# First routing of a two-layer mixture-of-experts kernel: one group of tiles per stage instead of one group per step, unrolled

## The chip, the cores and the metric

One core of one Trainium2 chip. The metric is device time in microseconds (us) of one execution. Engines: TensorE (PE; its weight loads are PEld), VectorE (DVE), ScalarE (ACT), GpSimd (POOL), and SyncE (SP), which only issues DMAs here. A trailing q (SPq, POOLq) is the queue of that engine.

## What is computed

```python
x = x + conv7x7_depthwise(ln_c(x))             # 16 x 128 x 24 x 24
t = tokens(x)                                  # 9216 tokens of 128
t = t + moe_0(ln_t(t))                         # 8 experts, top 2, 128 -> 512 -> 128, silu
x = x + filtered_leaky_relu(ln_c(from_tokens(t)))   # FIR up by 2, leaky ReLU, FIR down by 2
t = t + moe_1(ln_t(tokens(x)))                 # 8 experts, top 2, gated, 128 -> 256 -> 128

def moe_0(x):                                  # x: tokens x 128
    top_logits, top_idx = top_k(x @ Wg, 2)
    w = softmax(top_logits)                    # 2 weights per token
    return sum over the 2 experts e: w_e * silu(x @ W1[e]) @ W2[e]
```

The change concerns how `moe_0` finds, for every token, its two experts and its two rows in a table sorted by expert.

## The kernel before

Six stages follow each other, each behind a barrier of all engines: the first convolution, the first routing (`route0_phase`), the experts of layer 0, the second convolution with the second routing woven in (`conv1_phase`), the experts of layer 1, and the sum of the answers. The first routing is the stage between about 255 and 545 us of the trace.

It handles 20 **groups** of tokens (`GROUPS`): 4 image groups `ig` times 5 strips `q`, group number g = 5 ig + q. A group is 120 partitions (96 for q = 4) times 4 tiles of 128 features. The work on one group:

- SP loads it with one DMA per image row (L677): 5 of 48 KB, 4 where q = 4. The groups 0 to 4 are loaded first, then the constants `factor_a`, `factor_b`, `down`, `down_b` and the weights `w1l`, `w` (L682, L382, L383), then the groups 5 to 19. Group g waits until group g-5 is normalised.
- **measure**, DVE, L404 to L409: mean and variance. ACT takes the root (L416).
- **apply**, DVE, L424, L478, L431: reciprocal, the copy of the destinations into the row buffer `xn`, and the normalised rows. `xn` has 5 places, one per q, so group g waits until the scatters of group g-5 have landed (`scattered`). ACT copies the rows for the second expert (L489).
- **transposes and logits**, PE L498, ACT L507, PE L517.
- **pick**, DVE, L529 to L540: the two largest logits, their indices (L532), a cast of the indices to floats in `at` (L535), the one-hot form (L536), `picked` (L538). `gap` (L533) goes to ACT, which takes its exponential (L548). A different table is loaded by ACT for the root and for the exponential (ACT_TABLE_LOAD). PE then ranks the tokens (L557 to L561).
- **place**, DVE, L571 to L582: weights and row numbers (`slot`); its last act, at L583, frees POOL.
- POOL **scatters** the group: 8 DMA_INDIRECT instructions (L594), one per tile and choice.

What sets the order is the order of writing on each in-order engine. In step g DVE does measure g, pick g-1, apply g, place g-1, and each engine runs 5 steps as a loop body (`groups`: step 0 to 4 written out, then a loop over `ig`). Every DVE instruction that reads what the one ahead of it wrote waits on a semaphore that this one raises (`Chain`). After the last step DVE computes `factor_a` (L756), places the last group, makes the table of blocks (`route_make_table`, L610 to L638), and computes `down` (L759), `gl` (L761) and `w1l` (L763). ACT copies `w1h` (L710) and `gh` (L712) after its last step.

`conv1_phase` uses the same functions `norm_measure`, `norm_scale`, `norm_apply` and `route_pick`.

Of the kernel before, what the change touches and what calls it, by code (L numbers as in the profile page):

```python
# [28 lines left out]
P = 128  # L29
# [12 lines left out]
NORM_STEPS, PICK_STEPS, PLACE_STEPS = 3, 6, 4  # L42
# [344 lines left out]
class Norm:  # L387


    def __init__(self, nc, ctx, sem, name, eps):  # L390
        sb = lambda n, s: ctx.enter_context(nc.sbuf_tensor(f"{name}_{n}", s, F32))
        self.nc, self.eps = nc, eps
        self.stats, self.mv = sb("stats", [P, IG, 6]), sb("mv", [P, IG, 2])
        self.rstd = sb("rstd", [P, IG])
        self.chain, self.beat = sem(f"{name}_chain"), sem(f"{name}_beat")
        self.var_ready, self.std_ready, self.applied = (sem(f"{name}_{n}") for n in ("var", "std", "applied"))


def norm_measure(m, dve, ig, q, x):

    nc, px, g = m.nc, pixels(q), QT * ig + q
    ch = Chain(dve, m.chain, NORM_STEPS * g)
    for t in range(IG):
        ins = nc.vector.bn_stats(m.stats[0:px, t, :], x[:, t, :])  # L404
    ch.after(ins, m.beat)
    for t in range(IG):
        ins = nc.vector.bn_aggr(m.mv[0:px, t, :], m.stats[0:px, t, :])
    ch.after(ins)
    nc.vector.tensor_scalar(m.rstd[0:px], m.mv[0:px, :, 1], m.eps, None, ALU.add).then_inc(m.var_ready, 1)  # L409


def norm_root(m, act, ig, q):

    px = pixels(q)
    need(act, m.var_ready, QT * ig + q + 1)
    m.nc.scalar.activation(m.rstd[0:px], m.rstd[0:px], ACT.Sqrt).then_inc(m.std_ready, 1)  # L416


def norm_scale(m, dve, ig, q):

    nc, px, g = m.nc, pixels(q), QT * ig + q
    ch = Chain(dve, m.chain, NORM_STEPS * g + 2)
    need(dve, m.std_ready, g + 1)
    ch.after(nc.vector.reciprocal(m.rstd[0:px], m.rstd[0:px]))  # L424


def norm_apply(m, dve, ig, q, out, x):

    px = pixels(q)
    for t in range(IG):  # L430
        ins = m.nc.vector.tensor_scalar(out[:, t, :], x[:, t, :], m.mv[0:px, t, 0:1], m.rstd[0:px, t:t + 1],  # L431
# [4 lines left out]
class Router:  # L436


    def __init__(self, nc, ctx, sem, r, layer, xs):
# [3 lines left out]
        self.norm = Norm(nc, ctx, sem, f"ln{layer}", 1e-5)  # L443
# [3 lines left out]
        self.at, self.gap, self.ex, self.den = sb("at", [P, CHOICES]), sb("gap", [P, IG]), sb("ex", [P, IG]), sb("den", [P, IG])  # L447
# [74 lines left out]
def route_pick(ro, dve, ig, q):  # L522
# [8 lines left out]
    for t in range(IG):  # L531
# [124 lines left out]
def route0_phase(nc, io, r, wt, xs, src):  # L656

    with ExitStack() as ctx:
        sem = ctx.enter_context(stage_semaphores(nc, "r0_"))
        ro = Router(nc, ctx, sem, r, 0, xs)  # L660
# [7 lines left out]
        LAST = (IMAGE_GROUPS - 1, QT - 1)  # L668
# [20 lines left out]
        def _(act):  # L689
# [9 lines left out]
            def step(ig, q):  # L699
                last = before(ig, q)  # L700
                norm_root(ro.norm, act, ig, q)
                if last:
                    route_exponent(ro, act, *last)
                route_copy_rows(ro, act, ig, q)
                route_copy_turned(ro, act, ig, q)
# [17 lines left out]
        def _(pe):  # L723
# [3 lines left out]
            def step(ig, q):  # L727
                last = before(ig, q)
                if last:
                    route_ranks(ro, pe, *last)  # L730
# [661 lines left out]
```

## Time and profile before

| | us |
|---|---|
| median of the timed runs | 1649.24 |
| lowest and highest of the 3 runs | 1646.86, 1649.58 |
| span of the profiled execution | 1726.5 |
| GpSimd busy in it | 699.3 |
| VectorE busy in it | 1106.1 |
| TensorE busy in it | 1207.4 |

The page of the profile describes one execution, whose span runs from the first to the last instruction. It is 77.3 us longer than the median of the timed runs. Idle time of an engine is put down to the event that came last before the engine went on; "issue" and "remote" are waits for which the trace shows no releasing instruction, and a name such as `c_meanw` beside such a wait is that of an older owner of the same semaphore. Rows give the start and the duration in us; "x4" says that four like instructions are merged.

### The profile page before, as it was taken

What the parts mean: (1) busy time and instruction counts of PE and PEld (TensorE: products, weight loads), DVE (VectorE), ACT (ScalarE), POOL (GpSimd) and SP (SyncE); (2) the same over time, 40 slices, a digit from 0 to 9 for tenths busy, and PEclk for the clock granted to TensorE, in tenths of its full rate; (3) what the DMA queues carried; (4) which work ended last, traced back from release to release, by engine and by line L of the source; (5) the groups of instructions that cost most, each with busy time, mean ns of one, the idle gap of its engine ahead of it and who ended that gap; (6) DMA issues with size and microseconds to landing.
All of it is one profiled execution on the core that took longest, in us unless ns stands there. A gap on an engine that the chain in (4) does not pass through costs nothing. (4 is left out here: it accounts for less than half of the span.)

```text
span 1726.5 us, 31708 instructions
## 1 busy us (share of the span) xinstructions
PE 1207.4 (70%) x6568; PEld 956.4 (55%) x6569; DVE 1106.1 (64%) x4125; ACT 587.5 (34%) x1099; POOL 699.3 (41%) x680
## 2 busy tenths in 40 slices
PE   4799903223222999999946979889797089999940
PEld 4799902212122999998934545455454067777730
DVE  7677704434345666666648688787876467777754
ACT  4233303323231444444432234334344134444320
POOL 0100005565574444444434045345554535555530
PEclk9899955555555999999976989989898589999975
DMA  4033297121111222222232011121011122222239
GB/s 200 22 107 106 64 121 273 53 58 55 39 44 46 66 62 62 62 63 60 62 128 79 1 46 51 28 58 42 26 32 31 40 73 74 75 79 71 73 103 261
DMA packets 139200, 129.26 MB, mean 75 GB/s; under 512 B 56291, under 2 KB 119012, under 8 KB 138214
## 3 DMA queue, kind: packets, MB, share of 16 engines
q1 hardware_dynamic: 89396, 79.76, 16.9%
q0 software_dynamic: 19968, 39.44, 7.0%
q10 hardware_dynamic: 29778, 9.45, 2.7%
q14 instruction: 41, 0.34, 0.1%
q8 instruction: 17, 0.28, 0.1%
HBM read 78.66 MB, written 50.99 MB: 75 GB/s over the span
## 5 line engine op out<-in xcount | busy, mean ns | idle before, releaser
L594 POOL DMA_INDIRECT routed<-r_xn,r_slot x320 | 333.3, 1042 | 346.6 <-DVEq L583 233.9
L823 POOL DMA_INDIRECT answers<-e_y,e_dest x304 | 291.1, 958 | 347.1 <-ACT e_y L922 272.9
L972 DVE COPY e_ht<-e_ps_ht 128x512 f32<-128x512 f32 (+1 forms) x304 | 169.5, 558 | 180.9 <-PE e_ps_ht L859 156.7
L867 PE MATMUL e_ps_y<-w,e_ht 128*128 x1824 | 258.6, 278 | 13.4 <-DVE e_ht L972 7.4
L867 PEld LDWEIGHTS e_ps_y<-w,e_ht 128*128 128x128 f32 x1824 | 228.6, 192 | 20.1 <-issue 18.8
L1135 PE MATMUL c_pz<-c_c,down 116*120 116x512 f32 (+1 forms) x392 | 199.7, 627 | 0.0
L922 ACT ACTIVATE e_y<-e_ps_y,e_weight 128x128 f32<-128x128 f32 x304 | 111.8, 368 | 217.7 <-issue 117.9
L859 PE MATMUL e_ps_ht<-ident,e_h 128*128 128x128 f32 x912 | 150.8, 274 | 6.0 <-DVE e_h L958 5.5
L849 PE MATMUL e_ps_h<-w1h,e_xl 128*128 x308 | 150.9, 490 | 1.1 <-issue 0.7
L1109 PE MATMUL c_py<-c_xh,gl 121*116 121x512 f32 (+1 forms) x196 | 124.1, 633 | 39.1 <-DVE c_xl L1215 27.1
L859 PEld LDWEIGHTS e_ps_ht<-ident,e_h 128*128 128x128 f32 x912 | 115.4, 141 | 56.0 <-DVE e_h L958 10.7
L557 PE MATMUL r_ps_rank<-r_picked,before 120*120 120x32 bf16 (+1 forms) x40 | 9.9, 248 | 177.7 <-DVEq L539 150.1
L842 PE MATMUL e_ps_x<-ident,e_xg 128*128 128x128 f32 x310 | 86.0, 277 | 67.3 <-DMA e_xg<-routed 67.3
L1171 ACT ACTIVATE c_a<-c_py 116x512 f32<-116x512 f32 x116 | 69.0, 595 | 184.9 <-PE c_py L1109 159.0
L851 PE MATMUL e_ps_h<-w1h,e_xh 128*128 x308 | 123.5, 401 | 0.0
L850 PE MATMUL e_ps_h<-w1l,e_xh 128*128 x308 | 122.8, 399 | 0.0
L1223 DVE SCALAR_TENSOR_TENSOR c_c<-c_a 116x512 f32<-116x512 f32 x116 | 86.9, 749 | 52.1 <-ACT c_a L1171 41.1
L917 ACT ACTIVATE e_h<-e_ps_h 128x512 f32<-128x512 f32 x154 | 92.0, 597 | 61.1 <-PE e_ps_h L851 60.5
L557 PEld LDWEIGHTS r_ps_rank<-r_picked,before 120*120 120x120 bf16 (+1 forms) x40 | 6.1, 152 | 186.3 <-DVEq L539 155.3
L498 PE MATMUL r_ps_t<-ident,r_xn 120*128 120x120 f32 (+1 forms) x160 | 35.0, 362 | 95.3 <-DVE r_xn L431 83.3
L1135 PEld LDWEIGHTS c_pz<-c_c,down 116*120 116x120 f32 (+1 forms) x392 | 70.2, 187 | 52.5 <-issue 43.6
L950 DVE TENSOR_TENSOR e_xl<-e_ps_x,e_xh 128x128 fp32r<-128x128 f32 x310 | 90.3, 291 | 10.7
(134 smaller groups left out, 2445.4 us busy)
## 6 DMA issues: line engine op xcount, KB each, us to landing
e_xg<-routed SPq DMA_DIRECT2D x318, 66.0 KB
answers<-answers SPq DMA_DIRECT2D x32, 480.0 KB
c_w<-in_w SPq DMA_DIRECT2D x32, 448.0 KB
c_x<-in_xh SPq DMA_DIRECT2D x4, 1536.0 KB
routed<-r_xn,r_slot POOLq DMA_INDIRECT x320
answers<-e_y,e_dest POOLq DMA_INDIRECT x304
x<-x SPq DMA_DIRECT2D x96, 48.0 KB
w1l<-in_w SPq DMA_DIRECT2D x2, 2048.0 KB, 10.3
```

The source lines that it names most:

```text
L594: ro.nc.gpsimd.indirect_dma_start(ro.xs, bass.IndirectOffsetOnAxis(ap=ro.slot[0:px, q, c:c + 1], axis=0), ro.xn[0:px, q, k, t, :], None).t ...
L823: nc.gpsimd.indirect_dma_start(ys, bass.IndirectOffsetOnAxis(ap=dest[:, s:s + 1], axis=0), y[:, s, :], None).then_inc(stored[s], 16)
L849: nc.tensor.matmul(ps_h[i][:], xl[:, i, :], wt.w1h[:, bass.ds(w, FF)], start=True, stop=False)
L850: nc.tensor.matmul(ps_h[i][:], xh[:, i, :], wt.w1l[:, bass.ds(w, FF)], start=False, stop=False)
L851: nc.tensor.matmul(ps_h[i][:], xh[:, i, :], wt.w1h[:, bass.ds(w, FF)], start=False, stop=True).then_inc(h_ready, 1)
L859: ins = nc.tensor.transpose(ps_ht[s % 2][:, c * P:(c + 1) * P], h[:, s % 2, c * P:(c + 1) * P], r.ident[:])
L867: ins = nc.tensor.matmul(ps_y[s % 2][:, 0:P], ht[:, s % 2, c * P:(c + 1) * P], wt.w2[:, bass.ds(w + c * P, P)], start=c == 0, stop=c == ch ...
L917: nc.scalar.activation(h[:, i, :], ps_h[i][:], ACT.Silu).then_inc(hid_ready, 1)
L922: nc.scalar.activation(y[:, s % U, :], ps_y[s % 2][:, 0:P], ACT.Copy, scale=weight[:, s % U:s % U + 1]).then_inc(y_ready, 1)
L972: nc.vector.tensor_copy(ht[:, s % 2, :], ps_ht[s % 2][:, 0:HID]).then_inc(ht_ready, 1)
L1109: ins = nc.tensor.matmul(out, w[0:k, wcols], v, start=start and n == 0, stop=stop and n == 2)
L1135: ins = nc.tensor.matmul(ps_z[q % 3][0:rows, :], r.down[0:PPX, m * TPX:m * TPX + rows], c[0:PPX, p % R, :], start=p == ROWS * q, stop=p == ...
```

## The change

The steps of the stage are written out, 24 of them (20 groups and 4 to empty the pipeline), for every engine but SP, and in turn n each part works on another group: measure n, apply n-1, place n-4, pick n-3 on DVE; root n, copies of n-1, exponential of n-3 on ACT; transposes of n-1, logits of n-2, ranks of n-3 on PE. Since measure now runs a group ahead of apply, the norm's `mv` and `rstd` have two places in the first routing. The constants and weights are computed inside turns 12 to 14 instead of after the last step. In both routings the cast into `at` is gone: the one-hot form compares with the integer indices, in a view of 4 dimensions. The reciprocal of the norm has a semaphore of its own.

```diff
-        self.stats, self.mv = sb("stats", [P, IG, 6]), sb("mv", [P, IG, 2])
-        self.rstd = sb("rstd", [P, IG])
+        self.stats, self.mv = sb("stats", [P, IG, 6]), sb("mv", [P, ring, IG, 2])
+        self.rstd = sb("rstd", [P, ring, IG])
...
-    ch.after(nc.vector.reciprocal(m.rstd[0:px], m.rstd[0:px]))
+    nc.vector.reciprocal(m.rstd[0:px, i], m.rstd[0:px, i]).then_inc(m.inverted, 1)
+    need(dve, m.inverted, g + 1)
...
-    ch.after(nc.vector.tensor_copy(ro.at[0:px].rearrange("p (t k) -> p t k", k=2), ro.top_at[0:px, :, 0:2]))
-    ch.after(nc.vector.tensor_tensor(ro.onehot[0:px].rearrange("p t k e -> p (t k) e"), ro.r.iota8[0:px],
-                                     ro.at[0:px].unsqueeze(2).to_broadcast([px, CHOICES, EXPERTS]), ALU.is_equal))
+    ch.after(nc.vector.tensor_tensor(ro.onehot[0:px], ro.r.iota8[0:px].rearrange("p (t k) e -> p t k e", k=2),
+                                     ro.top_at[0:px, :, 0:2].unsqueeze(3).to_broadcast([px, IG, 2, EXPERTS]), ALU.is_equal))
...
+        APPLY, LOGITS, PICK, PLACE = 1, 2, 3, 4
+        WEIGHTS_AT = 12
+        def lagged(n, lag):
+            return [divmod(n - lag, QT)] if 0 <= n - lag < GROUPS else []
...
         @block.scalar
...
-            groups(act, step)
-            route_exponent(ro, act, *LAST)
-            act.wait_ge(w_in, 32)
-            nc.scalar.activation(wt.w1h[:], wt.w1f, ACT.Copy).then_inc(w_split, 1)
-            act.wait_ge(g_ready, 1)
-            nc.scalar.activation(r.gh[:], fa[:], ACT.Copy).then_inc(gh_ready, 1)
+            for n in range(GROUPS + PLACE):
+                for ig, q in lagged(n, 0):
+                    norm_root(ro.norm, act, ig, q)
+                for ig, q in lagged(n, APPLY):
+                    route_copy_rows(ro, act, ig, q)
+                    route_copy_turned(ro, act, ig, q)
+                for ig, q in lagged(n, PICK):
+                    route_exponent(ro, act, ig, q)
+                if n == WEIGHTS_AT:
+                    act.wait_ge(w_in, 32)
+                    nc.scalar.activation(wt.w1h[:], wt.w1f, ACT.Copy).then_inc(w_split, 1)
+                if n == WEIGHTS_AT + 1:
+                    act.wait_ge(g_ready, 1)
+                    nc.scalar.activation(r.gh[:], fa[:], ACT.Copy).then_inc(gh_ready, 1)
...
         @block.gpsimd
...
-            groups(pool, lambda ig, q: route_scatter(ro, pool, ig, q))
+            for n in range(GROUPS):
+                route_scatter(ro, pool, *divmod(n, QT))
...
         @block.tensor
...
-            groups(pe, step)
-            route_ranks(ro, pe, *LAST)
+            for n in range(GROUPS + PLACE):
+                for ig, q in lagged(n, APPLY):
+                    route_turn(ro, pe, ig, q)
+                for ig, q in lagged(n, LOGITS):
+                    route_logits(ro, pe, ig, q)
+                for ig, q in lagged(n, PICK):
+                    route_ranks(ro, pe, ig, q)
...
         @block.vector
...
-            groups(dve, step)
-            route_pick(ro, dve, *LAST)
-            dve.wait_ge(factors_in, 64)
-            nc.vector.scalar_tensor_tensor(fa[:], fa[:], 4.0, fb[:], ALU.mult, ALU.mult).then_inc(g_ready, 1)
-            route_place(ro, dve, *LAST)
+            for n in range(GROUPS + PLACE):
+                for ig, q in lagged(n, 0):
+                    need(dve, x_in[q], 16 * (pixels(q) // SIDE) * (ig + 1), ro.norm.beat)
+                    norm_measure(ro.norm, dve, ig, q, r.x[0:pixels(q), QT * ig + q])
+                for ig, q in lagged(n, APPLY):
+                    norm_scale(ro.norm, dve, ig, q)
+                    route_normalise(ro, dve, ig, q)
+                for ig, q in lagged(n, PLACE):
+                    route_place(ro, dve, ig, q)
+                for ig, q in lagged(n, PICK):
+                    route_pick(ro, dve, ig, q)
+                if n == WEIGHTS_AT:
+                    dve.wait_ge(w_split, 1)
+                    nc.vector.tensor_tensor(wt.w1l[:], wt.w1f, wt.w1h[:].bitcast(F32), ALU.subtract)
+                    dve.wait_ge(factors_in, 64)
+                    nc.vector.scalar_tensor_tensor(fa[:], fa[:], 4.0, fb[:], ALU.mult, ALU.mult).then_inc(g_ready, 1)
+                    nc.vector.tensor_tensor(r.down[:], r.down[:], down_b[:], ALU.mult)
+                if n == WEIGHTS_AT + 2:
+                    dve.wait_ge(gh_ready, 1)
+                    nc.vector.tensor_tensor(r.gl[:], fa[:], r.gh[:].bitcast(F32), ALU.subtract)
             route_make_table(ro, dve)
...
```

Two places in the order of DVE's instructions. The first is its start in the stage, before: measure 0 (above the piece), apply 0, measure 1, pick 0 (from L529), and, a few rows on, place 0 (from L571), which frees the first scatter.

```order
L424 RECIPROCAL ln_rstd<-ln_rstd 120x4
L478 COPY r_xn<-dest 120x8
L431 TENSOR_SCALAR r_xn<-x,ln_mv,ln_rstd 120x128 x4
L404 BN_STATS ln_stats<-x 120x6 x4
L407 BN_AGGR ln_mv<-ln_stats 120x2 x4
L409 TENSOR_SCALAR ln_rstd<-ln_mv 120x4
L529 MAX r_top<-r_ps_l 120x8 x4
L532 MAX_INDEX r_top_at<-r_top,r_ps_l 120x8 x4
L533 TENSOR_TENSOR r_gap<-r_top 120x4
L535 CAST r_at<-r_top_at 120x8
```

In the changed kernel the same pick 0 (L536 to L546 there) stands behind measure 0 to 3 and apply 0 to 2, and measure 4 (96 partitions) and apply 3 stand between it and place 0 (from L577); the piece begins at the end of pick 0.

```order
L546 TENSOR_REDUCE r_group_sum<-r_picked 120x8
L410 BN_STATS ln_stats<-x 96x6 x4
L413 BN_AGGR ln_mv<-ln_stats 96x2 x4
L415 TENSOR_SCALAR ln_rstd<-ln_mv 96x4
L430 RECIPROCAL ln_rstd<-ln_rstd 120x4
L485 COPY r_xn<-dest 120x8
L438 TENSOR_SCALAR r_xn<-x,ln_mv,ln_rstd 120x128 x4
L577 TENSOR_SCALAR r_den<-r_ex 120x4
L580 TENSOR_TENSOR r_earlier<-r_earlier,r_group_sum 120x8
```

So place 0 moved behind three more measures and two more applies, and place 1 now stands behind measure 5. The second place is the end of turn 12 on DVE, after: behind pick 9 stand the three long instructions that before came after the last step, and then measure 13.

```order
L546 TENSOR_REDUCE r_group_sum<-r_picked 96x8
L766 TENSOR_TENSOR w1l<-w1l,w1h 128x4096
L768 SCALAR_TENSOR_TENSOR factor_a<-factor_a,factor_b 128x1624
L769 TENSOR_TENSOR down<-down,down_b 128x1200
L410 BN_STATS ln_stats<-x 120x6 x4
```

Place 9 comes only after them, in turn 13.

## Rows read from the trace of the kernel before

**Rows 1.** The page's summary line.
```profile
span 1726.5 us, 31708 instructions
```

**Rows 2.** Groups of instructions by line, POOL, 255 to 545 us: busy, mean ns, idle before.
```profile
L594 POOL DMA_INDIRECT routed<-r_xn,r_slot x160 | 166.5, 1040 | 111.5 <-issue 59.9 <-DVEq L583 51.2 <-DMA routed<-r_xn,r_slot 0.3
```

**Rows 3.** Timeline of POOL: start, duration; in brackets idle before and releaser.
```profile
273.52 1.18 POOL L594 DMA_INDIRECT routed<-r_xn,r_slot  x1 [13.61 <-issue]
...
284.20 0.99 POOL L594 DMA_INDIRECT routed<-r_xn,r_slot  x1 [0.30 <-issue]
...
312.05 0.99 POOL L594 DMA_INDIRECT routed<-r_xn,r_slot  x1 [6.83 <-DVEq L583]
```

**Rows 4.** Timeline of DVE, the first steps of the stage.
```profile
264.36 0.87 DVE L404 BATCH_NORM_STATS2 ln_stats<-x 120x6 f32<-120x128 f32 x4 [0.35 <-DMA x<-x]
...
265.79 0.17 DVE L409 TENSOR_SCALAR ln_rstd<-ln_mv 120x4 f32<-120x4 f32 x1
267.77 0.39 DVE L529 MAX8 r_top<-r_ps_l 120x8 f32<-120x8 f32 x4 [1.81 <-PE r_ps_l L517]
...
269.01 0.17 DVE L535 CAST r_at<-r_top_at 120x8 f32<-120x8 uint32 x1
...
269.94 0.17 DVE L424 RECIPROCAL ln_rstd<-ln_rstd 120x4 f32<-120x4 f32 x1
...
271.24 0.16 DVE L571 TENSOR_SCALAR r_den<-r_ex 120x4 f32<-120x4 f32 x1
...
272.26 0.17 DVE L582 CAST r_slot<-r_slot_f 120x8 int32<-120x8 f32 x1
...
279.50 0.17 DVE L582 CAST r_slot<-r_slot_f 120x8 int32<-120x8 f32 x1
```

**Rows 5.** Timeline of DVE, a later step, while POOL issues its second group in a row.
```profile
403.73 0.38 DVE L407 BATCH_NORM_AGGREGATE ln_mv<-ln_stats 120x2 f32<-120x6 f32 x4 [2.44 <-DMA c_meanw<-in_mean_w]
408.53 0.17 DVE L409 TENSOR_SCALAR ln_rstd<-ln_mv 120x4 f32<-120x4 f32 x1 [4.43 <-DMA c_meanw<-in_mean_w]
```

**Rows 6.** SP's register instructions of line L677: duration ns min/median/max, first and last start.
```profile
L677 SPq FUSED_REGOPS  x72: 4/64/707, 272.5 to 446.7; - x72
```

**Rows 7.** Timeline of SP: the loads of the groups from 5 on, issued behind the weights.
```profile
272.83 54.12 SPq L677 DMA_DIRECT2D x<-x  x29
```

**Rows 8.** Stretches: length, busy PE, PEld, DVE, ACT, POOL, PEclk, DMA share, GB/s.
```profile
288.00:292.00 4.00, 2.69 (x12) 2.22 (x12) 0.29 (x2) 2.32 (x3) 3.00 (x4) 0.50 0.93 295
292.00:296.00 4.00, 0.00 (x0) 0.00 (x0) 1.33 (x7) 0.00 (x0) 2.81 (x3) 0.50 0.36 97
```

**Rows 9.** Timeline of PE and ACT in the second step of the stage.
```profile
272.48 0.57 ACT L507 ACTIVATE r_xnt<-r_ps_t 128x480 f32<-128x480 f32 x1 [0.49 <-PE r_ps_t L498]
...
273.10 1.77 PE L517 MATMUL r_ps_l<-wg,r_xnt 128*120 128x8 f32 x8 [0.66 <-ACT r_xnt L507]
...
274.58 1.28 ACT L548 ACT_TABLE_LOAD   x1
...
276.31 0.20 ACT L548 ACTIVATE r_ex<-r_gap 120x4 f32<-120x4 f32 x1 [0.45 <-DVE r_gap L533]
```

**Rows 10.** Timeline of all engines at the end of the stage.
```profile
510.88 3.60 ACT L710 ACTIVATE w1h<-w1l 128x4096 fp32r<-128x4096 f32 x1
...
511.62 1.84 DVE L756 SCALAR_TENSOR_TENSOR factor_a<-factor_a,factor_b 128x1624 f32<-128x1624 f32 x1
...
529.53 1.39 DVE L759 TENSOR_TENSOR down<-down,down_b 128x1200 f32<-128x1200 f32 x1
530.21 7.60 POOL L594 DMA_INDIRECT routed<-r_xn,r_slot  x1 [0.31 <-issue]
...
530.84 1.83 DVE L761 TENSOR_TENSOR gl<-factor_a,gh 128x1624 fp32r<-128x1624 f32 x1
532.60 4.41 DVE L763 TENSOR_TENSOR w1l<-w1l,w1h 128x4096 fp32r<-128x4096 f32 x1
```

**Rows 11.** Who waited for whom, second convolution and routing, 895 to 1385 us: total, times, longest.
```profile
PE r_ps_rank L557 <- DVEq L539: 29.7, 9, 9.4
```

More of the change, by code:

```diff
@@ L41 @@
 DEST, WEIGHT = P, P + 1
-NORM_STEPS, PICK_STEPS, PLACE_STEPS = 3, 6, 4
+NORM_STEPS, PICK_STEPS, PLACE_STEPS = 2, 5, 4
 CGS, CIN, RPAD = 4, 32, 32
@@ L406, in norm_measure @@
     for t in range(IG):
-        ins = nc.vector.bn_aggr(m.mv[0:px, t, :], m.stats[0:px, t, :])
+        ins = nc.vector.bn_aggr(m.mv[0:px, i, t, :], m.stats[0:px, t, :])
     ch.after(ins)
-    nc.vector.tensor_scalar(m.rstd[0:px], m.mv[0:px, :, 1], m.eps, None, ALU.add).then_inc(m.var_ready, 1)
+    nc.vector.tensor_scalar(m.rstd[0:px, i], m.mv[0:px, i, :, 1], m.eps, None, ALU.add).then_inc(m.var_ready, 1)
 def norm_root(m, act, ig, q):
-    px = pixels(q)
+    px, i = pixels(q), norm_slot(m, QT * ig + q)
     need(act, m.var_ready, QT * ig + q + 1)
-    m.nc.scalar.activation(m.rstd[0:px], m.rstd[0:px], ACT.Sqrt).then_inc(m.std_ready, 1)
+    m.nc.scalar.activation(m.rstd[0:px, i], m.rstd[0:px, i], ACT.Sqrt).then_inc(m.std_ready, 1)
 def norm_scale(m, dve, ig, q):
     nc, px, g = m.nc, pixels(q), QT * ig + q
-    ch = Chain(dve, m.chain, NORM_STEPS * g + 2)
+    i = norm_slot(m, g)
     need(dve, m.std_ready, g + 1)
-    ch.after(nc.vector.reciprocal(m.rstd[0:px], m.rstd[0:px]))
+    nc.vector.reciprocal(m.rstd[0:px, i], m.rstd[0:px, i]).then_inc(m.inverted, 1)
+    need(dve, m.inverted, g + 1)
 def norm_apply(m, dve, ig, q, out, x):
-    px = pixels(q)
+    px, i = pixels(q), norm_slot(m, QT * ig + q)
     for t in range(IG):
-        ins = m.nc.vector.tensor_scalar(out[:, t, :], x[:, t, :], m.mv[0:px, t, 0:1], m.rstd[0:px, t:t + 1],
+        ins = m.nc.vector.tensor_scalar(out[:, t, :], x[:, t, :], m.mv[0:px, i, t, 0:1], m.rstd[0:px, i, t:t + 1],
                                            ALU.subtract, ALU.mult)
@@ L446, in __init__ @@
         self.top, self.top_at = sb("top", [P, IG, 8]), sb("top_at", [P, IG, 8], U32)
-        self.at, self.gap, self.ex, self.den = sb("at", [P, CHOICES]), sb("gap", [P, IG]), sb("ex", [P, IG]), sb("den", [P, IG])
+        self.gap, self.ex, self.den = sb("gap", [P, IG]), sb("ex", [P, IG]), sb("den", [P, IG])
         self.onehot, self.picked = sb("onehot", [P, IG, 2, EXPERTS]), sb("picked", [P, IG, EXPERTS], BF16)
@@ L725, in _ @@
             pe.wait_ge(init, 2)
[L727 to L730, printed above, removed]
-                route_turn(ro, pe, ig, q)
-                route_logits(ro, pe, ig, q)
-            groups(pe, step)
-            route_ranks(ro, pe, *LAST)
+            for n in range(GROUPS + PLACE):
[5 more added lines that the diff above has]
+                    route_ranks(ro, pe, ig, q)
             route_count_all(ro, pe)
@@ L740, in _ @@
             nc.vector.tensor_copy(r.before[:], before_f[:]).then_inc(init, 1)
-            def step(ig, q):
-                last = before(ig, q)
-                need(dve, x_in[q], 16 * (pixels(q) // SIDE) * (ig + 1), ro.norm.beat)
-                norm_measure(ro.norm, dve, ig, q, r.x[0:pixels(q), bass.ds(QT * ig + q, 1)].rearrange("p a t c -> p (a t) c"))
-                if last:
-                    route_pick(ro, dve, *last)
-                norm_scale(ro.norm, dve, ig, q)
-                route_normalise(ro, dve, ig, q)
-                if last:
-                    route_place(ro, dve, *last)
@@ L762, in _ @@
-            dve.wait_ge(w_split, 1)
-            nc.vector.tensor_tensor(wt.w1l[:], wt.w1f, wt.w1h[:].bitcast(F32), ALU.subtract)
+            for n in range(GROUPS + PLACE):
[18 more added lines that the diff above has]
+                    nc.vector.tensor_tensor(r.gl[:], fa[:], r.gh[:].bitcast(F32), ALU.subtract)
```

26 lines of the change are left out of this document (9 added, 17 removed).

## The prediction

> **What bounds the kernel now.** I read the summary first. The profiled span is 1726.5 us [rows 1], the median of the timed runs 1649.24, so the profiled execution is 77.3 us longer than a timed one. An offset of that size matters here: somewhere it holds waits that a timed run may not have, and I had to find where before costing anything.
>
> Then the groups of instructions of the stage that the change rewrites. POOL issues 160 scatters of 1.04 us, and is idle for 111.5 us ahead of them, 51.2 of these for the release by DVE at L583 [rows 2]. The timeline of POOL shows the pattern: eight scatters take 284.20 - 273.52 = 10.7 us for the first group and 8 x (0.99 + 0.30) = 10.3 for a later one, I take 10.4; two groups run back to back, and then POOL stands idle, 6.83 us the first time, until DVE has placed the next [rows 3]. There are 8 such waits (51.2 us, 6.4 each).
>
> Why is DVE late? Its own step is short: place 0 ends at 272.43 and place 1 at 279.67, a step of 7.24 us [rows 4], 3 us less than POOL needs for a group. But while POOL issues its second group in a row, each wait of DVE stretches: 2.44 and 4.43 us on waits whose releaser had long been done [rows 5]. It is not DVE's data. SP, which touches no data, shows the same: register instructions with a median of 64 ns take up to 707 [rows 6]. So in those stretches every sequencer is slow, whatever it does.
>
> Are these stalls in the timed runs? Without them POOL would run through: 273.5 + 20 x 10.4 = 481.5, plus about 9 us in which long instructions of DVE hold it up (below), is 490.5. In the trace the last scatter ends at 530.21 + 7.60 = 537.8 [rows 10]. The stalls cost this stage 47.3 us, and 77.3 have to go somewhere. That is the only candidate of the right size that I find, and the slow waits look like something that comes with recording every instruction. I take it that **in a timed run the first routing is bound by POOL**, which issues without a gap from 273.5 on, and that DVE, PE and ACT have slack of 3 us per group. This is the assumption on which the sign rests.
>
> **The change part by part.**
>
> *The start (adds).* Before, DVE does measure 0, apply 0, measure 1, pick 0, apply 1, place 0. After, place 0 stands in turn 4, behind three more measures and two more applies. From the rows [rows 4]: measure 265.96 - 264.36 = 1.60; apply 271.24 - 269.94 = 1.30; pick 269.94 - 267.77 = 2.17, less the cast 0.20, is 1.97; place 272.43 - 271.24 = 1.19; from there to the first scatter 273.52 - 272.43 = 1.09 [rows 3, 4]. Measure 1 starts at 264.36, when group 1 has come. Turns 1 to 3 then end at 267.26, 270.16 and 275.03, and DVE reaches place 0 at 277.93. Place 0 also needs its exponential: ACT does that behind the copy of the transposed rows, which waits for logits 1, which wait for pick 0. From 275.0: 1.8 for the logits, 0.6 for the copy and 0.1 to wake it, 1.28 for the table, 0.2 for the exponential [rows 9] give 279.0. So place 0 ends at 280.3 and the first scatter starts at 281.4 instead of 273.5: +7.9 us. The bounds are +6.8 without that wait and about +9.
>
> *The second group (adds).* Turn 5 begins with measure 5, and place 1 stands behind it. Group 5 is loaded after the constants and weights (group 5 is issued from 272.83 on [rows 7]), 2 x 812 + 2 x 600 + 2 x 2048 KB, nearly 7 MB. The DMA engines are 93% busy with 295 GB/s from 288 to 292 and 36% with 97 after it [rows 8]; group 5 comes behind the weights in the same queue, so it lands at about 291, with 288 and 292 as bounds. Place 1 then ends at 291 + 1.60 + 1.30 + 1.19 = 295.1, and its first scatter starts at 296.2. Before, it started at 284.20 [rows 3], because measure 5 stood only ahead of place 4. POOL finishes group 0 at 291.8 and waits. **Everything behind shifts by 296.2 - 284.2 = +12.0 us**; this holds the +7.9, it doesn't add to it. With the load at 288 it is +9.0, at 292 +13.0.
>
> *Steady turns (nothing).* DVE's turn is 1.60 + 1.30 + 1.19 + 1.97 = 6.1, some 7 with the wait for the exponential, which each turn has too. POOL's group of 10.4 covers it. One margin shrinks: apply n-1 needs the places of group n-6 and stands ahead of place n-4, so POOL has one placed group ahead of it instead of three. Landing of n-6, about 1 us after POOL starts n-5, plus apply and place is 3.5 to 4 us, against 10.4. What DVE saves in a turn is worth nothing while POOL is the bound.
>
> *Constants and weights (moves).* `w1l` 4.41, `factor_a` 1.84, `gl` 1.83 and `down` 1.39, 9.5 us together [rows 10], move from the end to turns 12 to 14. POOL's last scatter took 7.60 us instead of 0.92 and ended 0.8 us after `w1l` [rows 10]: while such an instruction runs, POOL doesn't finish a scatter. In a timed run POOL is busy during them in either kernel, so it pays the same 9 us in the middle as at the end: 0. In turn 12 DVE is behind by 3.6 for ACT's `w1h` [rows 10] and 7.64 for three of them, so place 9 comes about 18 us after place 8 instead of 10.4; POOL has what is left of one group and all of another, and is itself held for 7.6: it just covers.
>
> The Trainium skill (SBUF — State Buffer, Who interferes with whom) says the same of the mechanism: DVE and GpSimd share a port pair under an exclusive lock, and a DVE instruction with two SBUF inputs shuts out a GpSimd one that reads SBUF. The row with 7.60 us agrees. By it a move within a busy POOL gains nothing.
>
> *The cast (removes).* In the first routing it is hidden. In the second PE waits for `picked` 9 times [rows 11], and each would come 0.2 us sooner: -1.8, I take -2. Bounds: 0 if the conversion costs the same inside the one-hot form, -4 for all 20 groups.
>
> *Sum:* 12.0 - 2.0 = +10.0 us. The profiled execution contains the stalls, so I set the difference against the median: **1649.2 + 10.0 = 1659 us**. Its own range is 1649.2 + (6.8 - 4) to 1649.2 + 13 = 1652 to 1662.
>
> **The rivals.**
>
> *The stalls are in the timed runs too (faster, or nothing).* For it: nothing in the trace says that they aren't; the 77 us could lie elsewhere. Against it: the size. Then DVE decides whenever POOL has run out. After a stall DVE did pick, apply and place before POOL went on; now apply and place are enough, 2 us less at 8 waits: -16. At the end the last scatter is not held: -6.7. Against these +12.0 at the start, up to +11.2 for the weights in turn 12, now on DVE's path (3.6 + 7.64), and -2 for the cast. Sum -1.5, between -20 (the weights hidden in a stall, the start partly) and +8: 1648, 1629 to 1657. It decides from the point where the stalls of a timed run keep DVE's step above 10.4 us.
>
> *Group 5 isn't late (slower, but less).* If in a timed run the load lands before 286, only the first term counts: +7.9 - 2 = 1655. The fill of DMA queues speaks against it.
>
> *The weights in turn 12 tear a hole (slower, more).* If POOL isn't held by them where they stand now, POOL empties its lead and waits up to 7 us: 1666.
>
> *The change doesn't shorten the turn at all.* By the wait for the exponential, DVE's turn is about 7 against 7.24. In the forecast this costs nothing; in the first rival it takes back some of the -16 and is in its range.
>
> **How the numbers follow.** Forecast 0.55; stalls real 0.28; group 5 early 0.10; hole 0.07. A difference under 0.2% (3.3 us) is about what a measurement of this kernel can't tell from none. Slower: all of the forecast but a small part (0.52), 0.08 + 0.07 of the two others, 0.05 of the first rival: 0.72, less a little for what I don't see: 0.68. Faster: 0.13 of the first rival and some for the unseen: 0.19. Same: 0.13. The range leaves out the better part of the first rival below 1638 and the hole beyond 1665.
>
> **What the profile after would show.** The first scatter at about 281 instead of 273.5, the second group at about 296 with POOL idle for 4 us ahead of it; DVE's instructions of measure 5 waiting for the DMA of `x`; `w1l`, `factor_a` and `down` in one block in the middle, with one scatter of 7 to 8 us beside them, and none such at the end. If the stalls are a part of the recording, the profiled stage still shows stretched waits, the profiled span is again far above the median, and the difference of the spans need not be that of the medians. The prediction is wrong if a timed run of the stage isn't bound by POOL: then the time falls or stays.

## The result and the profile after

| | median us (lowest to highest), runs | ratio to before, 95% interval |
|---|---|---|
| before | 1646.09 (1643.26 to 1649.58), 9 | |
| after | 1652.06 (1649.43 to 1658.17), 9 | 1.0035, 1.0019 to 1.005 |

The changed kernel is slower by 0.35%, about 5.7 us (3.1 to 8.2). The forecast was +10.0 us. The sign is right and so is the place of the loss, and the time lies at the lower edge of the forecast's own range (1652 to 1662). The size isn't right: the difference is little more than half of the forecast one. As a time the forecast was 1659, 7 us above the measured 1652.06; 3.1 us of that are in its base, since the median of before was 1649.24 in the three runs that it had and is 1646.09 in the nine here.

First the summary of the changed kernel: its span, and the lines with the busy tenths of DVE and POOL in 40 slices.

```profile
span 1650.9 us, 31277 instructions
...
DVE  7677714547443666566649698788877478887754
...
POOL 0100002677772444444435056455554545555520
```

This span is 1.2 us below the median of its timed runs. The one of before, 1726.5 [rows 1], was 77 us above the median beside it. So the two profiles can't be subtracted from each other: their spans say 76 us faster, the timed runs 5.7 slower. POOL is busy in seven tenths of the slices that the first routing fills (the 7777); once it has begun, its longest wait is 4.5 us.

Next the timeline of POOL in the changed kernel: start, duration, and in brackets the idle time before and who ended it. It answers to [rows 3].

```profile
282.49 1.18 POOL L600 DMA_INDIRECT routed<-r_xn,r_slot  x1 [21.37 <-ACT r_xn L496]
...
291.75 0.99 POOL L600 DMA_INDIRECT routed<-r_xn,r_slot  x1 [0.30 <-issue]
297.26 0.99 POOL L600 DMA_INDIRECT routed<-r_xn,r_slot  x1 [4.52 <-DVEq L589]
298.56 0.99 POOL L600 DMA_INDIRECT routed<-r_xn,r_slot  x1 [0.30 <-issue]
...
373.49 4.23 POOL L600 DMA_INDIRECT routed<-r_xn,r_slot  x1 [0.30 <-issue]
378.02 1.45 POOL L600 DMA_INDIRECT routed<-r_xn,r_slot  x1 [0.30 <-issue]
...
384.72 0.93 POOL L600 DMA_INDIRECT routed<-r_xn,r_slot  x1 [1.34 <-DVEq L589]
...
497.45 0.92 POOL L600 DMA_INDIRECT routed<-r_xn,r_slot  x1 [0.30 <-issue]
```

The first group is at 282.49 (forecast 281.4), the second at 297.26 (forecast 296.2); the stage began 1.2 us later in this execution (its first load is issued at 256.4 us instead of 255.2). Behind that there is one slow scatter in the middle beside `w1l`, one small hole at 384.72, and none at the end. Here is what DVE does in the same stretches (same columns; compare [rows 4] and [rows 10]).

```profile
280.19 0.17 DVE L577 TENSOR_SCALAR r_den<-r_ex 120x4 f32<-120x4 f32 x1 [0.98 <-ACT r_ex L554]
...
292.32 0.87 DVE L410 BATCH_NORM_STATS2 ln_stats<-x 120x6 f32<-120x128 f32 x4 [8.63 <-DMA x<-x]
...
372.42 4.42 DVE L766 TENSOR_TENSOR w1l<-w1l,w1h 128x4096 fp32r<-128x4096 f32 x1 [7.32 <-ACT w1h L720]
376.76 1.84 DVE L768 SCALAR_TENSOR_TENSOR factor_a<-factor_a,factor_b 128x1624 f32<-128x1624 f32 x1
378.52 1.40 DVE L769 TENSOR_TENSOR down<-down,down_b 128x1200 f32<-128x1200 f32 x1
```

Place 0 waits 0.98 us for its exponential, and measure 5 waits 8.63 us for the load of group 5, with place 1 behind it. The waits of the stage, 255 to 545 us (total, times, longest), say who is late in the steady turns:

```profile
DVE r_xn L485 <- DMA routed<-r_xn,r_slot: 41.7, 11, 4.6
...
DVE ln_stats L410 <- DMA x<-x: 10.9, 3, 8.6
POOL routed L600 <- DVEq L589: 8.0, 9, 4.5
DVE w1l L766 <- ACT w1h L720: 7.3, 1, 7.3
```

DVE waits 41.7 us for scatters to land, POOL only 8.0 us for DVE, 4.5 of them in the one wait at 297.26. In the steady turns POOL decides. The 7.3 us ahead of `w1l` are a wait for ACT's `w1h`, for which the prediction had 3.6. SP's register instructions, 707 ns at worst in [rows 6], are now all short:

```profile
L688 SPq FUSED_REGOPS  x72: 64/64/93, 273.6 to 399.6; - x72
```

### The profile page after: what moved, and what is told of

Read it like the earlier page. It is cut to its first block and busy times, and to the rows that moved or that the text cites. A ratio compares the mean times of both kernels' runs of the same rounds, so it can differ in the third digit from the quotient of the medians.

```text
span 1650.9 us, 31277 instructions
## 1 busy us (share of the span) xinstructions
PE 1189.7 (72%) x6568; PEld 950.9 (58%) x6569; DVE 1098.8 (67%) x4085; ACT 584.4 (35%) x1095; POOL 699.7 (42%) x680
## 5 line engine op out<-in xcount | busy, mean ns | idle before, releaser
L505 PEld LDWEIGHTS r_ps_t<-ident,r_xn 120*128 120x128 f32 (+1 forms) x160 | 23.4, 189 | 177.6 <-DVE r_xn L438 122.5
L1233 DVE SCALAR_TENSOR_TENSOR c_c<-c_a 116x512 f32<-116x512 f32 x116 | 92.5, 797 | 41.0 <-ACT c_a L1181 34.2
L960 DVE TENSOR_TENSOR e_xl<-e_ps_x,e_xh 128x128 fp32r<-128x128 f32 x310 | 90.3, 291 | 10.7
L852 PEld LDWEIGHTS e_ps_x<-ident,e_xg 128*128 128x128 f32 x310 | 44.0, 142 | 83.3 <-DMA e_xg<-routed 83.0
```

What stands on the lines that cost most here:

```text
L852: nc.tensor.transpose(ps_x[s % 2][:, 0:P], xg[:, s % U, 0:P], r.ident[:]).then_inc(x_turned, 1)
```

## The experiments

The theory: the stage is bound by POOL; the order makes the second group 12 us late, and something gives part of them back. The rivals for that something: the cast is worth more than was taken; the weights cost less in the middle; the written-out loop is cheaper; the start costs less than it seems. And open from before: where do the stretched waits of the first profile belong?

The ratios below are to the kernel before, timed beside it on the same chip, with a 95% interval in brackets; a gain in us is the ratio times the median of before there. Four chips took part. On three of them (5, 12 and 2) the median of before was 1646 to 1652 us, on one (6) it was 1742 at one time and 1724 at another. These two groups are kept apart. The chip of the result isn't on record; its before, 1646 us, is like the three.

### The kernel before, profiled again

> The kernel before, unchanged, profiled once more. Theory (the stretched waits of the first profile are no part of a timed run): the profiled span comes near the median of the timed runs, about 1645 to 1655 us instead of 1726.5, SP's register instructions show none of about 700 ns in the first routing, POOL runs from about 273.5 us without the waits of 6.4 us, and its last scatter ends at about 488 us instead of 537.8. Rival (the stretched waits belong to this kernel's looped form and are in every execution): the span is again about 1720 us and there are again 8 waits of some 6.4 us on DVE.

Chip 6, 29 timed runs of before from 1728.75 to 1751.49 us, median 1742.35. The profile shows the stretched waits. POOL's waits between 255 and 545 us (total, times, longest), and SP's register instructions (min/median/max in ns):

```profile
POOL routed L594 <- issue: 59.4, 151, 13.7
POOL routed L594 <- DVEq L583: 54.5, 9, 8.1
```
```profile
L677 SPq FUSED_REGOPS  x72: 3/64/747, 271.4 to 446.6; - x72
```

So the theory as it was put fell: here the timed runs are as long as the profiled one, which holds the stretched waits. But its rival, that they belong to the kernel, fell too, on another chip:

> The kernel before, unchanged, for a profile on the chip of this call. If before takes about 1646 us here, theory (no stretched waits on such a chip, POOL bound from the first scatter on): first scatter at 273 to 275 us, second group at 284 to 286, last scatter's end at about 488 us instead of 537.8, no SP register instruction of about 700 ns. Rival (the profile itself stretches the looped kernel, and only the timed runs are quick): last scatter at about 535 us. If before takes about 1740 here, the profile is like the first one.

Chip 6 again: median 1723.93 us, the last scatter ends at 539.0 us, 1.2 after that of the first profile.

> The kernel before, for a profile on the chip of this call. Where before takes about 1646 us: theory (no stretched waits there, POOL bound throughout) first scatter at 273 to 275 us, last scatter's end at 487 to 489 us, no SP register instruction of about 700 ns. Rival: last scatter at about 535 us as in the first profile. Where before takes 1715 to 1745: as in the three profiles with stretched waits, 533 to 539 us.

Chip 12: median 1651.72 us, and the profile is this (summary line, group of the scatters of the stage, SP's register instructions, timeline of POOL):

```profile
span 1649.1 us, 31708 instructions
```
```profile
L594 POOL DMA_INDIRECT routed<-r_xn,r_slot x160 | 165.7, 1036 | 62.1 <-issue 61.8 <-DMA routed<-r_xn,r_slot 0.3
```
```profile
L677 SPq FUSED_REGOPS  x72: 64/64/93, 273.5 to 380.9; - x72
```
```profile
273.88 1.18 POOL L594 DMA_INDIRECT routed<-r_xn,r_slot  x1 [13.62 <-issue]
...
284.56 0.99 POOL L594 DMA_INDIRECT routed<-r_xn,r_slot  x1 [0.30 <-issue]
...
436.09 2.56 POOL L594 DMA_INDIRECT routed<-r_xn,r_slot  x1 [0.30 <-issue]
...
451.45 7.37 POOL L594 DMA_INDIRECT routed<-r_xn,r_slot  x1 [0.30 <-issue]
...
487.16 0.92 POOL L594 DMA_INDIRECT routed<-r_xn,r_slot  x1 [0.30 <-issue]
```

Here is the kernel before without the stretched waits. POOL has one idle time of 13.6 us ahead of its first scatter and then nothing but the 0.30 us between two; of the 51.2 us of waiting for DVE in [rows 2] nothing is left. Its last scatter ends at 488.1; the prediction's reconstruction said 490.5. The long instructions of DVE run at 436 and 450 to 458, since DVE is three placed groups ahead and done with its own work:

```profile
435.94 1.84 DVE L756 SCALAR_TENSOR_TENSOR factor_a<-factor_a,factor_b 128x1624 f32<-128x1624 f32 x1
...
450.47 1.39 DVE L759 TENSOR_TENSOR down<-down,down_b 128x1200 f32<-128x1200 f32 x1
451.79 1.83 DVE L761 TENSOR_TENSOR gl<-factor_a,gh 128x1624 fp32r<-128x1624 f32 x1
453.55 4.40 DVE L763 TENSOR_TENSOR w1l<-w1l,w1h 128x4096 fp32r<-128x4096 f32 x1
```

One check on what makes a scatter slow is in the first of the two profiles on chip 6: there the last scatter (531.81) is over before the long instructions behind the table begin, and it takes what any other takes.

```profile
531.81 0.93 POOL L594 DMA_INDIRECT routed<-r_xn,r_slot  x1 [0.30 <-issue]
```
```profile
537.27 4.41 DVE L763 TENSOR_TENSOR w1l<-w1l,w1h 128x4096 fp32r<-128x4096 f32 x1
```

The stretched waits go with the chip, as far as four chips can tell: 52 runs of before on chip 6 lie between 1712.56 and 1751.49 us, and 91 on the others between 1642.14 and 1656.02. What it is in that chip, no run shows.

### The changed kernel again

> The changed kernel, unchanged, on the chip of this call. The first experiments were on a chip where every execution of before took 1729 to 1751 us and the stretched waits were there; the result was measured on one where it took 1643 to 1650. Theory (stretched waits belong to a chip, and with them DVE decides when POOL goes on, as in the prediction's first rival; without them POOL decides): if before takes about 1740 here, the changed kernel is 5 to 20 us faster; if before takes about 1646, it is 3 to 8 us slower. Rival (the stretched waits only make everything longer, the difference stays): +3 to +8 us on either chip.

Chip 5: 1.0024 (1.0011 to 1.0037).

> The changed kernel, unchanged. Where before takes about 1646: 1.002 to 1.0035 as twice already. Where before takes 1715 to 1745 (the prediction's first rival: DVE decides when POOL goes on, the new order leaves less for DVE between two groups): 0.990 to 0.997, its last scatter at about 525 us instead of 533 to 539. Rival (the same +4 to +6 us there too): 1.002 to 1.004.

Chip 12: 1.0024 (1.001 to 1.0038), second group at 297.37 us instead of 284.56, end of the last scatter at 498.8 instead of 488.1:

```profile
281.61 1.18 POOL L600 DMA_INDIRECT routed<-r_xn,r_slot  x1 [21.46 <-ACT r_xn L496]
...
297.37 1.00 POOL L600 DMA_INDIRECT routed<-r_xn,r_slot  x1 [5.46 <-DVEq L589]
...
497.87 0.92 POOL L600 DMA_INDIRECT routed<-r_xn,r_slot  x1 [0.30 <-issue]
```

> The changed kernel, unchanged. On the chips where before takes 1646 to 1652 it stood at 1.0035, 1.0024 and 1.0024, and should again. Where before takes 1715 to 1745 (the prediction's first rival: DVE decides when POOL goes on, and the new order leaves less of DVE's work between two groups): 0.990 to 0.996, as its relatives with the weights at the end (0.9939 and 0.9946) and with groups 5 and 6 loaded first (0.9921). Rival (its weights in turn 12 are on DVE's path there and take that back): 0.998 to 1.003.

Chip 2: 1.0032 (1.0019 to 1.0045). With the result that is +4.0 to +5.7 us, four times. The changed kernel itself was never timed on chip 6, so whether it is faster there is open.

### Without the late load

Groups 5 and 6 loaded ahead of the weights:

```diff
-            groups(sp, load, load_weights)
+            for n in range(GROUPS):
+                if n == 7:
+                    load_weights()
+                load(*divmod(n, QT))
```

The piece also writes out SP's loop, which the change had left as a loop.

> The changed kernel with the loads of groups 5 and 6 ahead of the constants and weights. Theory (place 1 behind the load of group 5 costs 3 to 4 us): where before takes about 1646, the second group's first scatter at about 292 us instead of 297, and 0.9995 to 1.001 against before, as with the measure at the end of the turn (1.0003); where before takes 1715 to 1745, about 0.992 as before, within 3 us of the changed kernel in the same call. Rival (the load costs nothing in the end): equal to the changed kernel in both.

Measured 0.9986 (0.9973 to 0.9999) on chip 12, 6 us less than the changed kernel beside it. That is more than the 3 to 4 us expected, and a little below the range of ratios given. The timelines of POOL and of DVE:

```profile
290.63 1.00 POOL L600 DMA_INDIRECT routed<-r_xn,r_slot  x1 [0.30 <-issue]
291.93 1.00 POOL L600 DMA_INDIRECT routed<-r_xn,r_slot  x1 [0.30 <-issue]
```
```profile
289.94 0.87 DVE L410 BATCH_NORM_STATS2 ln_stats<-x 120x6 f32<-120x128 f32 x4
```

Measure 5 waits for nothing, and the second group (291.93) starts right behind the first. The measure at the end of the turn instead of at its head, loads as in the change:

```diff
             for n in range(GROUPS + PLACE):
-                for ig, q in lagged(n, 0):
-                    need(dve, x_in[q], ...)
-                    norm_measure(...)
                 ...
                 for ig, q in lagged(n, PICK):
                     route_pick(ro, dve, ig, q)
+                for ig, q in lagged(n, 0):
+                    need(dve, x_in[q], ...)
+                    norm_measure(...)
```

> The changed kernel with the measure of group n moved from the head of DVE's turn to its end, so that place 1 no longer stands behind the load of group 5. Theory (second group late by 12 us is what costs): the second group's first scatter comes at about 290 us, right behind the first group, instead of 297.3, and the kernel is 4 to 6 us faster than the changed one where the waits aren't stretched. Rival (the start is hidden by what comes later, and the loss is elsewhere): within 1 us of the changed kernel. With stretched waits the start counts less: 0 to 6 us.

Measured 1.0003 (0.999 to 1.0016) on chip 5, 3.5 us below the changed kernel, the second group at 290.9 us. It falls just short of the 4 to 6 us expected. Two different edits that keep place 1 from waiting for the load bring 3.5 and 6 us, and only one of them touches SP; the load is the cause. The other part, 7 us for the first scatter, stays in both (280.4 and 281.3 us instead of 273.9).

> The changed kernel with the loads of groups 5 and 6 issued ahead of the constants and weights instead of behind them. Theory (place 1 waits for the load of group 5 behind the weights, and this makes the second group late): measure 5 doesn't wait, the second group's first scatter comes right behind the first group, at about 291 us instead of 297.3, and the kernel is 3 to 6 us faster than the changed one (which stood at 1.0024 and 1.0035), as it was with the measure moved to the end of the turn (1.0003). Rival (moving the measure helped by something other than the load): within 1 us of the changed kernel.

Chip 6: 0.9921 (0.9891 to 0.9952), the lowest ratio there.

### The order alone

The kernel before with everything of the change but the order of the steps: loop written out, cast removed, weights and constants in steps 12 to 14.

> Everything of the change but the order: loop written out, cast taken out, weights and constants in steps 12 to 14, but the steps of the groups in the order of before (first scatter at about 273.5 us, no place behind the load of group 5). Theory (the order costs +12 us and the rest brings 6): -5 to -8 us against before where the waits aren't stretched, so about 1640. Rival (the order costs less than 12 us and the rest brings nothing): within 2 us of before. With stretched waits: the order's own gain is missing, so slower than the changed kernel by 5 to 15 us.

Measured 0.9968 (0.9953 to 0.9983) on chip 5, first scatter at 274.6 us, end of the last at 487.1 against 496.4 for the changed kernel on that chip. By the medians the order costs 1651.69 - 1643.80 = 7.9 us, by the ratios (1.0024 - 0.9968) x 1647.7 = 9.2, and the last scatter says 9.3; the theory had 12. This version beats both kernels. With the cast kept in it:

> The kernel before, its loop written out, with w1l, factor_a, down and gl moved to step 12 to 14; order of the groups as before, cast kept. Theory (POOL pays less for them in the middle than at the end, where nothing but the last scatter and the start of the next stage is left): -3 to -7 us against before without stretched waits. Rival (they cost the same, the missing 6 us are elsewhere): -1 to +2 us. With stretched waits: up to 10 us slower, since DVE decides, or 0 where a stretched wait hides them.

Measured 1.0006 (0.9994 to 1.0018). So the weights in the middle and the loop written out, taken together, give nothing in the old order (the theory had -3 to -7 us). What made the version above fast is the cast, 0.0038 x 1647.7 = 6 us. That each of the two is worth nothing by itself isn't shown. Against the profile of before on chip 12, its second group starts at 285.90 us instead of 284.56, and from there to the end of the last scatter it takes 202.4 us instead of 203.5, so that the end is where it was, 488.3 against 488.1.

> The changed kernel with the weights and constants (w1l, factor_a, down, gl) back behind the last place, as in before. Theory (POOL pays as much for them in the middle as at the end): within 2 us of the changed kernel, so +5 to +8 against before. Rival (in the middle they cost less than at the end, and this is where the missing 6 us are): 4 to 7 us slower than the changed kernel, so about +10 to +13 against before.

The changed kernel with them at the end, chip 6: 0.9939 (0.991 to 0.9968), some 10 us faster than before. Both ranges had it slower; they reckoned without stretched waits.

> The changed kernel with w1l, factor_a, down and gl back behind the last place; it was 0.61% faster than before where the waits were stretched, and the changed kernel itself has not been timed there. Theory where before takes about 1646 (POOL pays less for them in the middle than at the end): 2 to 5 us slower than the changed kernel, so 1.004 to 1.007. Rival (they cost the same at either place, as the prediction says): within 1.5 us of it, 1.002 to 1.004.

Chip 6 once more, so the comparison with the changed kernel can't be made: 0.9946 (0.9925 to 0.9966).

> The kernel before with the loop over the image groups of the first routing written out on ACT, POOL, PE and DVE, in the order of before. Theory (the first routing is bound by POOL's scatters, and the loop costs POOL one jump for each 4 groups): 0 to -2 us. Rival (the registers and jumps of the loop cost POOL, DVE or the stage's start several us, and writing it out gives them back in the changed kernel): -5 us or more.

0.9946 (0.9917 to 0.9975), chip 6 too: 9 us, the rival's value there. On the chips without stretched waits the loop was only written out together with the moved weights (1.0006 above).

### The cast

```diff
-    ch.after(nc.vector.tensor_copy(ro.at[0:px]..., ro.top_at[0:px, :, 0:2]))
-    ch.after(nc.vector.tensor_tensor(ro.onehot[0:px]..., ro.r.iota8[0:px],
-                                     ro.at[0:px]..., ALU.is_equal))
+    ch.after(nc.vector.tensor_tensor(ro.onehot[0:px], ro.r.iota8[0:px]...,
+                                     ro.top_at[0:px, :, 0:2]..., ALU.is_equal))
```

> The kernel before with the cast taken out of the pick in both routings, nothing else. Theory (the cast saves 0.2 us only where PE waits for the pick in the second routing): -2 us against before, between 0 and -4. Rival (most of the 6 us by which the changed kernel beats the forecast comes from the cast): -6 to -8 us.

0.9953 (0.9923 to 0.9984), chip 6: 8 us, the rival's value, with an interval from 3 to 13.

> The kernel before with the cast taken out of the pick, nothing else, as in b1_cast_only, which was 0.47% faster where the waits were stretched. Two kernels of the last call differ in the cast alone and stood at 1.0006 and 0.9968, 6 us apart, where the prediction took 2. Theory (the cast is worth more in the second routing than its own 0.2 us for each wait of PE): -4 to -7 us where before takes about 1646. Rival (the prediction's term of -2 holds, and the 6 us are scatter): -1 to -3 us.

0.9971 (0.9948 to 0.9994), chip 6.

> The kernel before with only the cast removed. Theory (the cast is the mis-sized term, worth 6 us instead of 2, nearly all of it in the second routing, where PE waits for the pick and the convolution behind it): 0.9955 to 0.9975 where before takes about 1646. Rival (its term of 2 us holds): 0.998 to 0.9995. Where before takes 1715 to 1745 it has been at 0.9953 and 0.9971, and should be there again.

0.9964 (0.9953 to 0.9974) on chip 12: 5.9 us (4.3 to 7.8), where the prediction took 2. It is in the second routing: the last scatter of the first starts at 487.23 us, with the cast at 487.16. Below, the stretch from the first to the last scatter of the second routing (window, length, then busy us and counts of PE, PEld, DVE, ACT, POOL, then PEclk, DMA share, GB/s), before, then without the cast:

```profile
944.80:1308.60 363.80, 295.87 (x1080) 173.23 (x1078) 295.75 (x1168) 136.82 (x225) 199.55 (x184) 0.87 0.16 42
```
```profile
946.30:1303.70 357.40, 288.81 (x1080) 169.85 (x1078) 291.07 (x1149) 137.11 (x225) 200.77 (x184) 0.90 0.16 43
```

It is 6.4 us shorter. The same 1080 matmuls are busy 7.1 us less, at a granted clock of 0.90 instead of 0.87. PE's idle time in the stretch, length less busy time, is 67.9 us before and 68.6 without the cast: it didn't shrink. The idle time ahead of the ranks that the pick ends, PE and PEld added up, first before, then without the cast:

```profile
  DVEq L539: 52.2, 26
```
```profile
  DVEq L538: 45.3, 24
```

PE and its weight loads wait for the same picks, so these sums hold most waits twice. Apart (total, times, longest), before and then without the cast:

```profile
PEld r_ps_rank L557 <- DVEq L539: 29.3, 15, 7.3
PE r_ps_rank L557 <- DVEq L539: 22.8, 11, 6.8
```
```profile
PEld r_ps_rank L556 <- DVEq L538: 25.6, 13, 7.0
PE r_ps_rank L556 <- DVEq L538: 19.8, 11, 6.5
```

The waits for the pick are 3.0 us shorter on PE and 3.7 on PEld.

Does it cost DVE's time or PE's wait? The cast stays, but is done behind the signal, and the one-hot form reads the integers as in the change:

```diff
     dve.sem_inc(ro.picked_ready, 1)
+    nc.vector.tensor_copy(ro.at[0:px]..., ro.top_at[0:px, :, 0:2]).then_inc(ro.chain, 1)
```

> The kernel before with the one-hot form reading the integers directly, as in the change, but the cast still done by DVE, right behind the signal that the pick is ready (its result is not used). DVE does all the work of before, PE no longer waits for the cast. Theory (what costs is PE's wait for the pick, 19 times in the second routing, and the lower granted clock that comes with it): nearly all of the cast-only gain, 0.996 to 0.9975 where before takes about 1650 us, and a second routing of 355 to 358 us instead of 361 to 364. Rival (DVE's own time is on the chain there: behind the pick it has PE's next results to take): 0.999 to 1.000, and 361 to 364 us. Where before takes 1715 to 1745: 0.9953 and 0.9971 were measured without the cast; theory the same, rival 1.000.

0.9972 (0.996 to 0.9984) on chip 5, the second routing in 355.0 us, and the same two views:

```profile
  DVEq L538: 37.6, 21
```
```profile
943.10:1298.10 355.00, 287.04 (x1080) 169.58 (x1078) 293.99 (x1168) 137.41 (x225) 200.72 (x184) 0.90 0.16 43
```

DVE does the work of before (293.99 us busy) and the kernel has 4.6 of the 5.9 us; the other 1.3 are within the intervals. So it isn't DVE's time that costs but that the signal to PE comes later.

## Why the prediction was right or wrong

**That POOL decides: right where it was tested, for a reason that was half wrong.** Without stretched waits POOL issues without a gap from 273.9 to 488.1 us on chip 12, and the timed runs of the result, 1646 us for before, are as short as the ones there. The reconstruction of 490.5 was 2.4 us long, in the main because it took 10.4 us for every group, where those of 96 rows take 9.8. But the stretched waits are not "something that comes with recording every instruction": on one chip they are in the profiles and the timed runs are 70 us and more longer, on three there is no trace of either. The first profile and the three times beside it can't have been from the same condition. The 77 us between them said so. That the timed runs were free of these waits was luck: had they come from a chip like chip 6, the same reasoning would have given the same forecast.

**The start, +7.9: right.** On chip 12 the first scatter moved from 273.88 to 281.61, +7.7.

**The second group, +12.0: right to 1 us.** 297.37 - 284.56 = +12.8 on chip 12, by the load of group 5 behind the weights, as written. On chip 5 it is 295.49 against 284.33 in the kernel with the cast behind the signal, whose order is that of before: +11.2.

**Steady turns, 0: right.** From the second group to the last scatter POOL's only wait for DVE above 0.3 us is the one of 1.34.

**The weights, 0: right to 2 us, by another picture.** Between the second group and the end of the last scatter the changed kernel takes 498.8 - 297.4 = 201.4 us, before 488.1 - 284.6 = 203.5. Summed over the stage, the scatters of before take 9 us more than their usual 0.99 or 0.92 us each, as the prediction took, nearly all of it beside DVE's long instructions. In the changed kernel it is 6 to 7 us, and 1 us of waiting besides. In the kernel before, the slow scatters lie 30 us and more ahead of the last scatter and not at the end, where [rows 10] had them. In the old order the same move, with the loop written out, gave nothing that could be timed (1.0006). The Trainium skill (SBUF — State Buffer, Who interferes with whom) has DVE and GpSimd exclude each other on a shared port. The scatter of 7.37 us beside `gl` and `w1l` agrees here too.

**The cast, -2: this is the step that failed.** It was sized as "PE waits for `picked` 9 times", from the row of a profile with stretched waits [rows 11], with 0.2 us for each. It measured 5.9 us (4.3 to 7.8) with the cast gone and 4.6 us (2.6 to 6.6) with it only behind the signal, so that it costs by making the signal later, as the prediction had it, but two to three times as much. The count was off by little: counted alike, PE alone, there are 11 such waits without stretched waits, and 15 of PEld. Even 20 x 0.2 = 4 us, which the prediction had kept as a bound and which takes all 20 picks of the second routing, is 2 us short of the 5.9.

Where the rest comes from isn't shown. The profiles put the whole gain into the matmuls, which ran at 0.87 before and at 0.90 without the cast, and none into PE's idle time. In eight of the nine profiles of kernels without the cast ahead of the signal (chips 5, 12 and 2 and the result) the clock of that stretch was 0.89 to 0.91; in the ninth it was 0.88 and the stretch took 360.3 us, about as long as the 361.0 of one of the two with the cast, at 0.88 too. The other of those two has 0.87. So the length of the stretch goes with the clock. But the clock can't be all of it: in the timed runs its mean over the whole execution rose from 0.844 to 0.848 on chip 12, while on chip 5 it was 0.848 both before and with the cast behind the signal, and the 4.6 us were there all the same. That less waiting causes the higher clock is likely and not shown.

With the terms at the sizes measured on chip 12 the sum is 12.8 - 2.1 - 5.9 = +4.8, against +4.0 there and +4.0 to +5.7 in all four. The 5.9 are from the old order; in the changed kernel the cast wasn't put back. What is left of the forecast's +12 at the last scatter is 10.7 us on chip 12, and the order alone costs 8 to 9 on chip 5, so the cast carries 3 to 4 us of the miss and this 1 to 4.

**The first rival, the stalls being real:** not so in the result. On chip 6 it has this for it: kernels with the new order wait less for DVE there. POOL's waits between 255 and 545 us in the changed kernel with the weights at the end, on chip 6 (the second of its two profiles):

```profile
POOL routed L600 <- DVEq L589: 39.0, 10, 5.9
```

Before had 54.5 and 54.2 us there. That is 15 us less, near the 16 that the rival took for it. But the cast alone and the loop alone, which the kernel with the new order also contains, gained nearly as much in time (0.9953, 0.9971, 0.9946), the changed kernel wasn't timed there, and so this rival is open on such a chip. **Group 5 not late:** wrong, it waits 8.63 us. **The hole:** 1 us of the 7, though `w1l` waited 7.3 us for ACT and not 3.6.

## What to carry to other kernels

When a profiled span stands nearly 5% above the median of the timed runs, the two were not taken in the same condition, and a wait read from that profile may not be in the timed runs. A small instruction ahead of a signal between two engines that take turns may cost more than itself: 0.2 us, 20 times, cost 4.6 and 5.9 us here, above the product of the two, and only the kernel without it could price it. Against this, moving 9.5 us of DVE's work to another place changed the time by 2 us at most, though at either place it held up POOL's scatters. And a software pipeline that puts a later group's load ahead of an earlier group's last step on the same engine ties the start to the slowest load: here that alone was 3.5 to 6 us. The old order with the cast removed is faster than either kernel (0.9964 and, with the weights moved, 0.9968).

## What the runs showed of the hardware

Chips differ by some 5% for one and the same kernel: 1646 to 1652 us on three, 1724 and 1742 on the fourth. On that one, SP's register instructions in the first routing take up to 747 ns instead of 93 at most, POOL waits 54 us for DVE instead of not at all, and the spread of 29 runs is 23 us instead of 9. A comparison made on one kind need not hold on the other: the changed kernel with the loads of groups 5 and 6 first stood at 0.9921 (0.9891 to 0.9952) on chip 6 and at 0.9986 (0.9973 to 0.9999) on chip 12, while the cast alone came out alike on both (0.9953 and 0.9971, 0.9964).

Scatters of POOL issued in a row start every 1.29 us for 120 rows and every 1.22 us for 96. Beside long DVE instructions with two inputs in SBUF a scatter takes longer: 7.37 us beside `gl` and `w1l` in a row (1.83 and 4.40 us), 4.23 beside `w1l` (4.42), and 1.42 to 2.56 beside ones of 1.4 to 1.8 us. Between 300 and 435 us of the profile on chip 12, where DVE runs none of that length, every scatter takes 0.92 to 1.00 us.
